# Two layer norms in a row computed in one stage: the second factor from the variance that the first measured

## The reference, cut to what matters

```
def _layernorm(x, axis=-1, eps=1e-05):
    m = jnp.mean(x, axis=axis, keepdims=True)
    v = jnp.var(x, axis=axis, keepdims=True)
    return (x - m) / jnp.sqrt(v + eps)
...
def _L3_gnn_ref(x, edge_weight, ln_w, ln_b, W, b, gamma, beta, edge_row, edge_col):
    mu = jnp.mean(x, axis=-1, keepdims=True)
    var = jnp.var(x, axis=-1, keepdims=True)
    h = (x - mu) * jax.lax.rsqrt(var + 1e-05) * ln_w + ln_b
    h = h * jax.nn.sigmoid(h)
    msg = edge_weight[:, None] * h[edge_col]
    z = jax.ops.segment_sum(msg, edge_row, num_segments=n_nodes)
    h = z @ W.T + b
    h = h * gamma + beta
    return x + h
...
x = x + _L3_gnn_ref(_layernorm(x, axis=-1), edge_weight, ...)
```

## Time and profile before

| | |
|---|---|
| time, median of 3 runs | 6384.12 us |
| the three runs | 6384.12, 6384.26, 6370.35 us |
| the profiled execution | 6370.07 us |
| its span in the profile | 6368.4 us |
| mean granted clock of TensorE | 0.831 |
| busy over the span | PE 75%, DVE 54%, ACT 27%, POOL 38% |
| `wsum_ln`: VectorE's first step to the last copy | 5373.83 to 5392.92 us |
| `wsum_ln2`: VectorE's first step to the last copy | 5393.54 to 5424.57 us |
| weighted sum: first gather to the last addition | 5461.28 to 6017.86 us |

### The profile page before, as it was taken

The page is one execution under the profiler, slowest core; times in us unless marked ns, Lnnn a source line. Parts: engine busy times, 40 slices in busy tenths (PEclk is TensorE's granted clock), DMA queues, the critical chain, the costliest instruction groups (busy, mean ns, idle before and its releaser), DMA issues. The chain is left out here.

```text
span 6368.4 us, 92114 instructions
## 1 busy us (share of the span) xinstructions
PE 4744.9 (75%) x23633; PEld 3321.9 (52%) x23634; DVE 3460.6 (54%) x6834; ACT 1720.4 (27%) x4054; POOL 2446.0 (38%) x2744
## 2 busy tenths in 40 slices
PE   5867879745569976766579789999999494455566
PEld 2213435634347743555456667777777352455545
DVE  8988983656752254999758622220112234555533
ACT  0955643411112243111100333332222222100022
POOL 0857965467328634777300000001111301577500
PEclk8998989855559988788679879999999697677678
DMA  0002447322210077999757100014332321233300
GB/s 30 2 10 111 170 150 245 124 33 35 53 34 15 1 258 295 339 322 320 204 174 236 26 15 10 15 45 127 99 101 80 87 99 51 87 101 101 74 15 20
DMA packets 400860, 686.92 MB, mean 108 GB/s; under 512 B 116697, under 2 KB 286574, under 8 KB 396166
## 3 DMA queue, kind: packets, MB, share of 16 engines
q1 hardware_dynamic: 302174, 428.98, 21.2%
q0 software_dynamic: 98304, 255.53, 13.2%
q10 hardware_dynamic: 192, 0.15, 0.0%
HBM read 451.45 MB, written 233.01 MB: 107 GB/s over the span
## 5 line engine op out<-in xcount | busy, mean ns | idle before, releaser
L3231 POOL CAST sagel_piece<-x 128x1600 fp32r<-128x1600 f16 (+1 forms) x75 | 112.3, 1498 | 1640.2 <-DMA x<-counts 1200.0
L511 POOL DMA_INDIRECT back_sorted<-back_space x391 | 397.0, 1015 | 334.2 <-issue 329.5
L928 POOL DMA_INDIRECT wsum_a_rows<-table,edge_src x416 | 417.5, 1004 | 220.1 <-issue 119.7
L942 PE MATMUL wsum_a_ps<-wsum_a_hot,wsum_a_rows 128*128 128x128 f32 x1664 | 316.6, 368 | 244.6 <-DMA wsum_a_rows<-table,edge_src 149.2
L2062 POOL DMA_INDIRECT big<-hgt_table,edge_key x448 | 423.6, 946 | 176.3 <-issue 110.7
L942 PEld LDWEIGHTS wsum_a_ps<-wsum_a_hot,wsum_a_rows 128*128 128x128 f32 x1664 | 290.9, 271 | 270.2 <-DVE big L969 193.5
L511 POOL DMA_INDIRECT own_sorted<-big x256 | 290.6, 1135 | 291.4 <-issue 290.5
L3287 PE MATMUL sagel_ps<-sagel_piece,sagel_high 128*128 128x512 f32 (+1 forms) x1050 | 399.6, 388 | 0.8 <-issue 0.8
L3287 PE MATMUL sagel_ps<-sagel_piece,sagel_low 128*128 128x512 f32 (+1 forms) x1050 | 380.1, 375 | 0.0
L2110 PE MATMUL hgt_s_pq<-big 128*128 x1344 | 248.8, 350 | 175.8 <-DVE hgt_s_tmp L2149 151.5
L716 PE MATMUL cnt_ps<-cnt_hot_s,cnt_hot_d 128*128 128x512 bf16 (+1 forms) x1792 | 324.4, 335 | 67.2 <-DVE cnt_hot_s L698 59.7
(11 more groups left out here) (987 smaller groups left out, 10925.3 us busy)
## 6 DMA issues: line engine op xcount, KB each, us to landing
hgt_edge_values<-big SPq DMA_DIRECT2D x112, 512.0 KB
big<-hgt_edge_values SPq DMA_DIRECT2D x112, 512.0 KB, 4.5
x<-counts SPq DMA_DIRECT2D x75, 400.0 KB, 3.1
x<-counts SPq DMA_DIRECT2D x75, 384.0 KB, 3.1
counts<-big SPq DMA_DIRECT2D x25, 832.0 KB
counts<-big SPq DMA_DIRECT2D x25, 768.0 KB
big<-counts SPq DMA_DIRECT2D x30, 640.0 KB, 6.6
counts_turned<-big SPq DMA_DIRECT2D x30, 640.0 KB
```

What stands on the lines that cost most here:

```text
L511: self.nc.gpsimd.indirect_dma_start(self.e.dram, bass.IndirectOffsetOnAxis(ap=self.adr[:, c:c + 1], axis=0), self.rec[:, c, :], None).then ...
L928: nc.gpsimd.indirect_dma_start(rows[n % DEEP][:, u, :], None, table, bass.IndirectOffsetOnAxis(ap=e.src[:, g:g + 1], axis=0)).then_inc(gat ...
L942: mm = nc.tensor.matmul(ps[r.slot % 2][u][:, k * P:(k + 1) * P], rows[r.slot][:, u, k * P:(k + 1) * P], hot[r.slot % 2][:, u, :], start=Tr ...
```

## The change

The two blocks become one, `layer_norm_twice`. It has these streams:

- VectorE: the same steps to the variance, now without eps in it; eps is added into `std` by an eighth step (L851). After the square root it takes the reciprocal `rstd` (L853), then forms v * rstd^2 + eps (L854 to L856), which is the variance of the normalized row plus eps, and the first norm's shift (L857). After a second square root it takes the reciprocal (L860) and multiplies it into `rstd2` and `shift2` (L861, L862). Each tile's `tensor_scalar` (L867) then goes from `x` straight to the twice normalized tile in `st`. It waits for `turned` of tile t - 5, no longer for ScalarE.
- ScalarE: both square roots (L873, L875). Then for each tile one ACTIVATE with the function Identity (L878), which computes the once normalized tile from `x` with `rstd` as scale and `shift` as bias (each one number a partition, read from memory) and writes it to `b1`; then, after `turned`, the copy of the PSUM bank to `b2` (L881).
- TensorE: the same two transposes a tile (L891), which now wait for `kept` of tile t - 5.

The loops are written out in full: no hardware loop, no register steps. The copy of the second norm to `b3` is gone, and so are the 25 `bn_stats` of the second norm and one barrier.

```diff
+def layer_norm_twice(nc, kit, nm, x, xn, xt, loads):
...
+                link(nc.vector.tensor_scalar(var[:], var[:], 1.0 / D, None, ALU.mult))
+                link(nc.vector.scalar_tensor_tensor(out=var[:], in0=tmp[:], scalar=0.25, in1=var[:],
+                                                    op0=ALU.mult, op1=ALU.add))
+                link(nc.vector.tensor_scalar(std[:], var[:], EPS, None, ALU.add))
+                dve.wait_ge(rooted, 1)
+                link(nc.vector.reciprocal(rstd[:], std[:]))
+                link(nc.vector.tensor_tensor(tmp[:], rstd[:], rstd[:], ALU.mult))
+                link(nc.vector.tensor_tensor(var[:], var[:], tmp[:], ALU.mult))
+                link(nc.vector.tensor_scalar(var[:], var[:], EPS, None, ALU.add))
+                link(nc.vector.scalar_tensor_tensor(out=shift[:], in0=mean[:], scalar=-1.0, in1=rstd[:],
+                                                    op0=ALU.mult, op1=ALU.mult))
+                dve.wait_ge(rooted, 2)
+                link(nc.vector.reciprocal(var[:], var[:]))
+                link(nc.vector.tensor_tensor(rstd2[:], rstd[:], var[:], ALU.mult))
+                link(nc.vector.tensor_tensor(shift2[:], shift[:], var[:], ALU.mult))
+                for t in range(NT):
+                    if t >= U:
+
+                        dve.wait_ge(turned, t - U + 1)
+                    nc.vector.tensor_scalar(st[t % U][:], nat(x)[:, t, :], rstd2[:, t:t + 1], shift2[:, t:t + 1],
+                                            ALU.mult, ALU.add).then_inc(normed, 1)
+
+            @block.scalar
+            def _(act):
+                act.wait_ge(step, 8)
+                nc.scalar.activation(std[:], std[:], ACT.Sqrt).then_inc(rooted, 1)
+                act.wait_ge(step, 12)
+                nc.scalar.activation(var[:], var[:], ACT.Sqrt).then_inc(rooted, 1)
+                act.wait_ge(step, 13)
+                for t in range(NT):
+                    nc.scalar.activation(nat(xn)[:, t, :], nat(x)[:, t, :], ACT.Identity, bias=shift[:, t:t + 1],
+                                         scale=rstd[:, t:t + 1]).then_inc(plain, 1)
+                    act.wait_ge(turned, t + 1)
+                    nc.scalar.copy(tr(xt)[:, :, t * P:(t + 1) * P], ps[t % U][:, 0:D].rearrange("p (k n) -> p k n", k=2)
+                                   ).then_inc(kept, 1)
+
+            @block.tensor
+            def _(pe):
+                for t in range(NT):
+                    pe.wait_ge(normed, t + 1)
+                    if t >= U:
+                        pe.wait_ge(kept, t - U + 1)
+                    for k in range(2):
+                        mm = nc.tensor.transpose(ps[t % U][:, k * P:(k + 1) * P], st[t % U][:, k * P:(k + 1) * P],
+                                                 kit.ident[:])
+                    mm.then_inc(turned, 1)
...
-            layer_norm(nc, kit, "wsum_ln", x, b1, b2, loads=loads, measured_before=True)
-        layer_norm(nc, kit, "wsum_ln2", b1, b3, b2)
+            layer_norm_twice(nc, kit, "wsum_ln", x, b1, b2, loads)
```

More of the change, by code:

```diff
@@ L824, in _ @@
                         nc.tensor.transpose(ps[u][:, P:D], st[u][:, P:D], kit.ident[:]).then_inc(turned, 1)
+def layer_norm_twice(nc, kit, nm, x, xn, xt, loads):
+    with ExitStack() as c:
+        mean, var, tmp, std, rstd, shift, rstd2, shift2 = (
+            c.enter_context(nc.sbuf_tensor(f"{nm}_{n}", [P, NT], F32))
+            for n in ("mean", "var", "tmp", "std", "rstd", "shift", "rstd2", "shift2"))
+        st = [c.enter_context(nc.sbuf_tensor(f"{nm}_st{u}", [P, D], F32)) for u in range(U)]
+        ps = [c.enter_context(nc.psum_tensor(f"{nm}_ps{u}", [P, 512], F32)) for u in range(U)]
+        step, rooted, normed, turned, kept, plain = sems(nc, c, nm, "step rooted normed turned kept plain")
+        with nc.Block() as block:
+            block.sync(loads)
+            @block.vector
+            def _(dve):
+                link, stats = link_on(dve, step), kit.stats
+                link(nc.vector.tensor_tensor(mean[:], stats[:, :, 1], stats[:, :, 4], ALU.add))
+                link(nc.vector.tensor_scalar(mean[:], mean[:], 0.5, None, ALU.mult))
+                link(nc.vector.tensor_tensor(tmp[:], stats[:, :, 1], stats[:, :, 4], ALU.subtract))
+                link(nc.vector.tensor_tensor(tmp[:], tmp[:], tmp[:], ALU.mult))
+                link(nc.vector.tensor_tensor(var[:], stats[:, :, 2], stats[:, :, 5], ALU.add))
+                link(nc.vector.tensor_scalar(var[:], var[:], 1.0 / D, None, ALU.mult))
[41 more added lines that the diff above has]
+                    mm.then_inc(turned, 1)
```

## The result

| | kernel before | changed kernel |
|---|---|---|
| median of six runs each, same chip | 6378.67 us | 6351.58 us |
| lowest to highest | 6370.35 to 6384.26 | 6347.54 to 6355.07 |
| profiled execution: time, span | 6370.07, 6368.4 us | 6350.41, 6348.7 us |
| granted TensorE clock, mean | 0.831 | 0.833 |
| first norm's first step to the next block's table load | 5373.83 to 5424.85, 51.02 us | 5380.43 to 5404.79, 24.36 us |

The ratio is 0.9956 with an interval of [0.9946, 0.9966]: 27.1 us less, with the interval 22 to 34. The forecast was 26.2 us less, with a range of 6338 to 6366 us.

A forecast was written before the change was run, and what follows sets the result against it. ScalarE was taken to bound the tile loop. The second block goes (31.65 us), 1.08 comes back in the head and 4.85 in the loop: 26.2 us less, from a median of 6384.12 to 6357.9 us, range 6338 to 6366.

The forecast's parts named there:

- The bound: Tile loop: ScalarE's two instructions a tile set the pace; TensorE (0.47 us a tile) and VectorE (0.41) keep up.
- VectorE runs up to five tiles ahead: Tile loop: VectorE and TensorE both run ahead of ScalarE by up to five tiles.
- VectorE's wait for `turned` is met early: Tile loop: VectorE's wait is met early, and only TensorE's wait for `kept`, 5 tiles back, holds.
- The head: Block's short steps before the first tile: seven more steps, a second root and a second reciprocal cost 1.08 us net.
- The pair: ScalarE in the tile loop: Identity 0.488 plus copy 0.285, so a pair takes 0.773 us.
- The rule of the Trainium skill: ScalarE's Identity and copy: by the rule the pair is 0.80 us and the block saves 25.5 instead of 26.2 us.
- The sum: Whole block: first bank copy at 5379.45, 24 intervals of 0.773, last copy 0.40, end at 5398.40; 26.2 us less.
- Its reach: Stages behind the block: their work is unchanged and each starts behind a barrier, so the whole 26.2 us reaches the end.
- Hidden operands: Rival, ScalarE's tile loop: Identity's operands cost nothing, pair stays at 0.57 us, 31.0 us less, 6353.1; chance 0.12.
- No overlap at 0.99: Rival, ScalarE's tile loop: Identity and copy do not overlap, pair 0.99 us, 21.0 us less, 6363.1; chance 0.16.
- Slower by the weighted sum: Rival, weighted sum: TensorE at its lower clock, matmuls and additions taking turns, 54 us slower, 6438; chance 0.03.
- the two places of the runs: Rival, whole time: runs fall at two places and cover the gain; median 12 us less, 6372; chance 0.06.

The follow-up runs named there:

- e0: Control on the first chip: the changed kernel with wait values masked to their range in two earlier stages; 6388.23 us, ratio to the kernel before 1.0018, block 24.40 us.

## Why the prediction was right

**The bound** (ScalarE's queue, TensorE and VectorE beside it) held: ScalarE waits once in the tile run. That VectorE runs up to five tiles ahead was too low a number: it may be five ahead of TensorE, and TensorE five ahead of ScalarE, and it did 13 tiles by 5389.26, when ScalarE was at its fifth bank. That VectorE's wait for `turned` is met early was wrong too, it waited 11 times and 4.1 us. Nothing hung on either.

**The head** was forecast with the first tile 4.28 us after the first step; measured 4.26. The steps came every 0.22, the roots and reciprocals where the earlier trace rows had put them, and the second root was hidden by the shift but for 0.11. The 1.08 us that the head was to cost net is less sure than it looked: it counts against the 0.93 of the loop's entry, which was an exception. Against the usual 0.58 it is 1.43, and 0.35 of the block's 26.66 is the chance of that one trace.

**The pair** was taken at 0.773 and came at 0.757 ((5404.05 - 5385.88) / 24), between bounds of 0.57 and 0.99. The Identity itself, derived from the nearest row as 0.488, took 0.50. The larger error is in the term beside it: I took the mean of two copies, 0.285, for the one that stays. The earlier trace rows had shown that the copy from SBUF takes 0.31 and the one from PSUM 0.26, and it is the cheaper one that stays. With 0.50 + 0.26 the pair would have been 0.76. That the pair came within 0.016 is in part luck: the Identity was 0.015 too low and the copy 0.03 too high. The same mean of two copies had spoilt the price of the scale. Line 580 against the SBUF copy of this width, 0.31 - 0.106 = 0.20, gives 0.292 - 0.20 = 0.09 and not 0.113, and 0.09 is what was measured.

**The rule of the Trainium skill** ("ScalarE: Activation LUTs", section "What ACT_TABLE_LOAD costs"), about 93 ns for each operand, agrees: 91 ns for the scale here and 92 for the shift with the change of function, in a full queue. The estimate for the pair by that rule, 0.80, does not, because by it every copy of this width is an estimated 0.306, which fits the one from SBUF (0.31) and not the one from PSUM (0.25 to 0.26).

**The sum.** From the first step to the end of the last copy I forecast 24.57 us (5398.40 - 5373.83) and it took 24.09 (5404.52 - 5380.43). By terms: head 0.02 less, the first tile to the first bank copy 0.15 less (1.19 for 1.34), 24 pairs 0.38 less, the last copy 0.07 more; together 0.48 less. The 1.34 had been read from a loop; with the loop put back it was 1.33. The block saved 26.66 us for 26.2, the medians 27.1; with an interval of 22 to 34 that the medians agree to 0.9 is luck, the block's number is not.

**Its reach.** "The whole 26.2 us reaches the end" holds to 0.36 us in one profiled pair (943.91 for 943.55 behind the block), as the sum of 1.5 less and 1.9 more in stages that do the same work.

**The rivals.** Hidden operands: excluded by the pair of 0.66 with one operand and 0.57 with none. No overlap at 0.99: excluded by 0.757. Slower by the weighted sum: the gathers and their issue are unchanged, TensorE's granted clock over them is 0.70 (0.71 before) and not the lower one throughout, and the stretch from the next table load to the block after the sum took 624.8 us (5404.79 to 6029.6) for 626.4.

**Wrong: the two places of the runs.** I read three runs as "two places where runs fall", 6384 and 6370, and gave a rival to it. Three more runs of the kernel before took 6375.56, 6373.62 and 6381.77, and 27 on one chip lie between 6368.65 and 6388.11 with no gap above 3.4 us. It is one broad scatter. In the pair compared above nearly all of the difference ahead of the block was there before 500 us. The forecast of 6357.9 stands 6.3 above the measured median, 5.5 of it because the median of before fell from 6384.12 to 6378.67 with more runs.

Still open: what scatters the early stages by 6 us from run to run; no run here was made for it.

## What to carry to other kernels

Where a block between two barriers has one engine without idle time, its time is the head plus tiles times the distance of that engine's starts, and a rewrite can be priced to half a microsecond from the distances in the timeline (not from the recorded durations, which overlap). Take the distance of each kind of instruction by itself, not the mean of a pair: the one that stays may be the cheaper. Then look for who reads the result: the kept norm had a single reader, an addition, and folding it into the scale was worth another 6.7 us in the profile (44.75 to 38.10), and sharing it with an engine that waits a further 5.7 (38.10 to 32.40).

## What the runs showed of the hardware

- A scale read from memory costs ScalarE 0.091 us at 128x256, and a bias (with Identity for Copy, which no run separates) 0.092, though the queue is full and neighbours overlap.
- In a full queue ScalarE's copy of 128x256 takes 0.31 us from SBUF and 0.25 to 0.26 from PSUM.
- VectorE's `tensor_scalar` of 128x256, 0.32 us apart alone, went 0.40 apart beside GpSimd working with constants and 0.57 beside GpSimd with operands from memory, each time at GpSimd's own distance, with no idle time recorded for it: the slowdown hides in the duration (481 and 648 ns for 408). GpSimd gave way by 0.03 us a tile (0.37 to 0.40 and 0.54 to 0.57).
- Entering the looped form of the tile run cost 0.36 us of VectorE's time here (0.58 for 0.23 to the first tile).
- A mask with an addition ahead of each of TensorE's waits cost 39 to 41 us in the HGT sums on the first and the third chip and 25 to 32 on the second (1650.9 and 1654.0 for 1622.4 and 1625.7), a mask alone next to nothing (1421.6 for the 1419.4 of before).
- Two of the chips differ by 6.6% on the same program (6378.1 and 6798.87 us). In the profiles the block is the same to 0.01 us (24.40 on both), and the stages without a gather agree within 2 us, as `soft_ln` to `sage_ln` with 618.2 and 619.2. Most stages with gathers do not, as `gat_ln` to `hgt_ln` with 981.7 us on the first (e0, 1250.4 to 2232.1) and 1106.8 on the second (1270.3 to 2377.1). What differs between the chips no run shows. The ratio of the change is 0.9956 in the first comparison and on the second chip.
- The first gather of the weighted sum took 7.23 us on POOL, those behind it 0.95, in both kernels. The first gathers of the other stages took 1.0 to 1.3 us; why this one is long is open.
